# Attention scores on Trainium2: stacked heads formed on TensorE, or spread through DRAM by DMA

## The reference

```
x = x + fusion(recurrent layers(layernorm(x)))
s = layernorm(x)
q, k, v = s @ Wq + bq, s @ Wk + bk, s @ Wv + bv        # 16 heads of 8 features
scores = einsum('bqhd,bkhd->bhqk', q, k) * 8 ** -0.5
probs = softmax(scores)
attn = einsum('bhqk,bkhd->bqhd', probs, v) @ Wo + bo
x1 = layernorm(s + attn)
expert = floor(x1 @ router_w + router_b) mod 4          # one of four experts per token
x = x + layernorm(x1 + expert's MLP(x1))
```

## Time and profile before

| | us |
|---|---|
| median of 3 runs | 369.08 |
| lowest and highest of them | 367.32, 375.83 |
| profiled execution, its own time | 369.33 |
| its span, first to last instruction | 367.5 |
| TensorE busy in the span | 272.2 |
| VectorE busy | 247.6 |
| ScalarE busy | 191.5 |
| GpSimd busy | 145.1 |

### The profile page before, as it was taken

One profiled execution on the slowest core, in us unless ns is written; L12 is line 12 of the kernel. 1 busy time (PEld: TensorE's weight loads), 2 busy tenths in 40 slices (PEclk: granted clock), 3 DMA queues, 4 the chain that ended last, 5 costly groups with the idle time before them and its releaser, 6 DMA issues. The chain is left out here.

```text
span 367.5 us, 7953 instructions
## 1 busy us (share of the span) xinstructions
PE 272.2 (74%) x2807; PEld 197.3 (54%) x2807; DVE 247.6 (67%) x664; ACT 191.5 (52%) x357; POOL 145.1 (39%) x333
## 2 busy tenths in 40 slices
PE   2654686877876838759888888988865898679970
PEld 1233454545555524546557566756755757447860
DVE  5997788888888592263538656866864377728881
ACT  4323969979978764633654654465341233214420
POOL 1126547657557360131003301820420152726665
PEclk9966869989988985966999999999976699969995
...
GB/s 152 239 332 336 320 61 0 1 2 0 0 3 2 110 4 2 0 0 2 2 2 4 3 2 2 61 4 0 62 75 0 2 90 31 73 125 58 25 23 19
DMA packets 19806, 20.46 MB, mean 56 GB/s; under 512 B 1554, under 2 KB 18224, under 8 KB 19640
## 3 DMA queue, kind: packets, MB, share of 16 engines
...
## 5 line engine op out<-in xcount | busy, mean ns | idle before, releaser
L1128 ACT ACTIVATE probs<-scores 128x1024 f32<-128x1024 f32 x32 | 32.8, 1025 | 54.7 <-PE scores L801 54.4
L1392 DVE TENSOR_REDUCE mneg<-scores 128x8 bf16<-128x1024 f32 x32 | 39.0, 1218 | 24.7 <-PE scores L794 22.2
L1256 DVE TENSOR_TENSOR_SCAN early<-a_both,bank 128x512 f32<-128x512 f32 x32 | 38.8, 1212 | 4.5 <-issue 4.0
L428 POOL TENSOR_SCALAR a_both<-early 128x508 f32<-128x508 f32 x32 | 19.6, 611 | 37.6 <-ACT early L1025 33.7
L1400 DVE RECIPROCAL sums<-bank 128x128 f32<-128x128 f32 x16 | 15.3, 957 | 23.5 <-PE bank L824 23.4
L648 PE MATMUL scores<-ident,early 128*128 128x128 f32 x64 | 16.6, 319 | 17.7 <-DVE early L1274 16.3
L609 PE MATMUL bank<-ident,early 128*128 128x128 f32 x136 | 25.3, 318 | 5.0 <-ACT h_fwd L1042 2.1
L801 PE MATMUL scores<-mnegT,pick 32*128 32x128 bf16 x256 | 27.8, 239 | 0.0
L453 POOL TENSOR_TENSOR ln_tmp<-ln_tmp,minus_half 128x8 f32<-128x8 f32 x16 | 26.4, 1650 | 1.3
L1025 ACT ACTIVATE early<-scores,gate_wT 128x512 f32<-128x512 f32 x28 | 19.9, 712 | 11.0 <-PE scores L635 3.7
L648 PEld LDWEIGHTS scores<-ident,early 128*128 128x128 f32 x64 | 10.2, 167 | 28.0 <-issue 28.0
...
...
...
## 6 DMA issues: line engine op xcount, KB each, us to landing
...
late<-sorted_rows SPq DMA_DIRECT2D x15, 130.0 KB, 2.1
x_rows<-in_x_dram SPq DMA_DIRECT2D x4, 256.0 KB, 3.4
w_s<-in_L_ffn_W_dram SPq DMA_DIRECT2D x1, 1024.0 KB, 6.2
w_s<-in_L_ffn_W_dram SPq DMA_DIRECT2D x4, 256.0 KB, 6.8
a_both<-in_L_ffn_b_dram SPq DMA_DIRECT2D x1, 1024.0 KB, 4.7
x_rows<-sorted_rows SPq DMA_DIRECT2D x4, 130.0 KB, 2.0
ctx_rows<-in_ctx_dram SPq DMA_DIRECT2D x1, 256.0 KB, 2.9
```

Source lines behind the costliest of these rows:

```text
L428: pool.tensor_scalar(a_buf[d][:, (k // 2) % 2, :, keep], tiles(keep_buf[:, i, :])[:, :, keep], CLAMP_HI, CLAMP_LO, ALU.min, ALU.max).then_ ...
L1128: act.activation(probs[:, n % 2, 1 - h::2, :].rearrange("p (j i) q -> p j i q", i=2), exp_banks.rearrange("p i j q -> p j i q"), ACT.Exp, ...
L1256: dve.tensor_tensor_scan(out_s, a, b, 0.0, ALU.mult, ALU.add).then_inc(s["s_ready"], 1)
L1392: dve.tensor_reduce(mneg[:, n % 2, h::2, 0:4], max_banks, AX.X, ALU.max, negate=True).then_inc(s["mx_r"], 1)
```

## The change

Groups 1 to 3: no stacks on TensorE and ScalarE. SP writes each of k_hi, k_lo, q_hi and q_lo twice to DRAM (256 KB each, eight DMAs a group), at the places that the four planes have them in, waits for the four of the keys to land, reads the key stacks back with one 1 MB DMA (`k_in`), then does the same for the queries (`q_in`). The last score step's first half of a group waits for both.

Group 0: no stacks. ScalarE writes the keys in fp32 (`k_cols`), VectorE writes four copies of the queries in fp32, each with all features but those of one of every four heads set to 0 (`q_own`, mask `own`). `maxima_of` and `score_step` read them through `operands`, so that in tiles 0 to 3 the matmuls of lines 794 and 797 are fp32 (those of the maxima of tile 4, made at tile 3, are not). A head then stands at another place, and `exp_half` writes the first four tiles in that order. The `sel` matrices, which ScalarE zeroed and VectorE filled, are gone, and the work ahead of the loop is in another order. The diff, with most of the unchanged lines left out:

```diff
@@ -100,7 +100,7 @@
-        sel = sb("sel", [P, 4, NHEAD // 4, P], F32R)
+        own = sb("own", [P, 4])
         ctx_rows = sb("ctx_rows", [P, LAYERS, P])
@@ -145,6 +145,7 @@
                       for i, n in enumerate(("q_st", "k_st")))
+        q_own, k_cols = sb("q_own", [P, 4, CHUNK]), sb("k_cols", [P, CHUNK])
         v_z = sb("v_z", [P, TPC * NHEAD * VW + 3 * (VW + HD)])
@@ -184,6 +185,7 @@
         table = nc.dram_tensor("sorted_rows", [ROWS, ROW], F32)
+        k_spread, q_spread = (nc.dram_tensor(n, [NG - 1, NHEAD // 4, P, CHUNK], F32) for n in ("key_stacks", "query_stacks"))
         blank = sb("blank", [P, ROW])
@@ -225,12 +227,13 @@
         names = """x_in0 x_in1 x_in2 x_in3 ctx_in vec_in fw_in rw_in attw_in bc_in b12_in w1_in w2_in out_done
-        ident_done pool_init sel_z vz_z mask_done x_norm x_rowsT x_cols prep_T prep_cols
+        ident_done pool_init vz_z mask_done x_norm x_rowsT x_cols prep_T prep_cols
         u_ready keep_r gated b_r decay s_ready rows_ready st_r ln_p coef n_dve n_act cols_ready h_ready dve1
         fus_p fus_s fusT_p x1_r xn_r xnT_p xnT_s q_p q_hi_r q_lo_r k_p k_hi_r k_lo_r v_p v_r
-        ks_p ks_act qs_p qs_act xnb_r x1b_r norm_st_r norm_p norm_co_r
+        xnb_r x1b_r norm_st_r norm_p norm_co_r
         sc_p mx_r mT_p mT_s st_p exp_r pv_p att_r bv_c bvo_p bo_r wo_p r1_r xh1_r xh1T_p xaT_s key_p mask_r
         blank_r blanked consts cum_r rank_p place_r scattered0 scattered1 scattered2 scattered3 steer_r
+        k0_r q0_r k_out k_in q_out q_in
         xsT_p xs_r hid_p hid_r hidT_p relu_r y_p acc_r acc_p acc_rs_r o_r dve2""".split()
@@ -393,6 +396,24 @@
             sp.dma_start(b1_bc, b1.rearrange("(o e) f -> o (e f)", o=1).to_broadcast([P, NE * DFF])).then_inc(s["b12_in"], 16)
+            def spread_rows(g, dram, whole, rest, whole_at, rest_at, whole_r, rest_r, out, into, stacks):
+                spread = dram.ap()[g - 1].rearrange("j (i b d) c -> b (j i) d c", i=4, b=4)
+                for src, planes, ready in ((whole, whole_at, whole_r), (rest, rest_at, rest_r)):
+                    sp.wait_ge(s[ready], g)
+                    for b in planes:
+                        sp.dma_start(spread[b], src[:, :].bitcast(F32)).then_inc(s[out], 16)
+                sp.wait_ge(s[out], 16 * 4 * g)
+                sp.dma_start(stacks[g % 2][:, :, :].bitcast(F32), dram.ap()[g - 1].rearrange("j p c -> p j c")).then_inc(s[into], 16)
+            for g in range(1, NG):
+                if g == 1:
+                    sp.wait_ge(s["h_ready"], LAYERS * STEPS)
+                else:
+                    sp.wait_ge(s["st_p"], HALVES * TPC * (g - 1))
+                spread_rows(g, k_spread, k_hi, k_lo, (0, 1), (2, 3), "k_hi_r", "k_lo_r", "k_out", "k_in", k_st)
+                spread_rows(g, q_spread, q_hi, q_lo, (0, 2), (1, 3), "q_hi_r", "q_lo_r", "q_out", "q_in", q_st)
             for i in range(NS):
@@ -697,7 +718,7 @@
                 if g:
-                    pe.wait_ge(s["qs_act"], 4 * g)
+                    wait(pe, "q_lo_r", g - 1)
                     pe.wait_ge(s["h_ready"], LAYERS * STEPS)
@@ -706,6 +727,7 @@
                 pe.wait_ge(s["fus_s"], g + 1)
+                wait(pe, "k_lo_r", g - 1)
                 for t in range(TPC):
@@ -723,35 +745,6 @@
                 pe.matmul(dst[:, :], wq_s[:, :], xnT[:, :], start=True, stop=True).then_inc(s["q_p"], 1)
-            def stack_bank(g, j):
-                return bank[j] if g == 0 else bank[7 - j % 2]
-            def stack_keys(g):
-                for j in range(4):
-                    if j == 0:
-                        pe.wait_ge(s["k_lo_r"], g + 1)
-                    if j == 1 or g == 0:
-                        pe.wait_ge(s["q_lo_r"], g + 1)
-                    if j >= 2 and g:
-                        pe.wait_ge(s["ks_act"], 4 * g + j - 1)
-                    for lo, src in enumerate((k_hi, k_lo)):
-                        last = pe.matmul(stack_bank(g, j)[:, :], sel[:, lo, j, :], src[:, :], start=(lo == 0), stop=(lo == 1))
-                    last.then_inc(s["ks_p"], 1)
-            def stack_queries(g):
-                for j in range(4):
-                    if g == 0:
-                        pe.wait_ge(s["ks_act"], j + 1)
-                    elif j < 2:
-                        pe.wait_ge(s["ks_act"], 4 * g + 3 + j)
-                    else:
-                        pe.wait_ge(s["qs_act"], 4 * g + j - 1)
-                    for lo, src in enumerate((q_hi, q_lo)):
-                        last = pe.matmul(stack_bank(g, j)[:, :], sel[:, 2 + lo, j, :], src[:, :], start=(lo == 0), stop=(lo == 1))
-                    last.then_inc(s["qs_p"], 1)
@@ -764,15 +757,22 @@
+            def operands(g, rows, j, at):
+                if g == 0:
+                    return q_own[rows, j, at], k_cols[rows, at]
+                return q_st[g % 2][rows, j, at], k_st[g % 2][rows, j, at]
             def maxima_of(n, h):
...
                 for j in range(4):
+                    pe.wait_ge(s["q0_r"], j + 1)
                     for i in range(2):
                         rows, at = head_rows(h, i, t)
-                        last = pe.matmul(max_banks[:, i, j, :], q_st[g % 2][rows, j, at], k_st[g % 2][rows, j, at],
-                                         start=True, stop=True)
+                        q, k = operands(g, rows, j, at)
+                        last = pe.matmul(max_banks[:, i, j, :], q, k, start=True, stop=True)
                 last.then_inc(s["sc_p"], 1)
@@ -785,17 +785,17 @@
                     if t1 == 0:
-                        pe.wait_ge(s["ks_act"], 4 * (g1 + 1))
-                        pe.wait_ge(s["qs_act"], 4 * (g1 + 1))
+                        pe.wait_ge(s["k_in"], 16 * g1)
+                        pe.wait_ge(s["q_in"], 16 * g1)
                 for j in range(4):
...
                             rows, at = head_rows(h, i, t1)
-                            top = pe.matmul(max_banks[:, i, j, :], q_st[g1 % 2][rows, j, at], k_st[g1 % 2][rows, j, at],
-                                            start=True, stop=True)
+                            q, k = operands(g1, rows, j, at)
+                            top = pe.matmul(max_banks[:, i, j, :], q, k, start=True, stop=True)
                         rows, at = head_rows(1 - h, i, t)
-                        pe.matmul(exp_banks[:, i, j, :], k_st[g % 2][rows, j, at], q_st[g % 2][rows, j, at],
-                                  start=True, stop=False)
+                        q, k = operands(g, rows, j, at)
+                        pe.matmul(exp_banks[:, i, j, :], k, q, start=True, stop=False)
                     for i in range(2):
@@ -876,19 +876,17 @@
             keys(0, bank[1])
-            queries(0, bank[0])
-            to_cols(LAYERS - 1, STEPS - 2)
-            to_cols(LAYERS - 1, STEPS - 1)
-            pe.wait_ge(s["mask_done"], 3)
-            stack_keys(0)
-            stack_queries(0)
+            queries(0, bank[3])
             pe.wait_ge(s["bv_c"], 1)
             pe.matmul(bank[4][:, 0:P], bv_cols[:, :], wo_s[:, :], start=True, stop=True).then_inc(s["bvo_p"], 1)
-            pe.wait_ge(s["qs_act"], 4)
+            to_cols(LAYERS - 1, STEPS - 2)
+            pe.wait_ge(s["k0_r"], 1)
             maxima_of(0, 0)
+            maxima_of(0, 1)
+            to_cols(LAYERS - 1, STEPS - 1)
+            turn_shift(0)
             fusion(1)
-            maxima_of(0, 1)
-            turn_shift(0)
+            pe.wait_ge(s["mask_done"], 2)
             pe.wait_ge(s["pool_init"], 8)
@@ -912,8 +910,6 @@
                     router(g - 1)
-                if t == 2 and g < NG - 1:
-                    stack_queries(g + 1)
                 if t == 3 and g < NG - 2:
@@ -924,8 +920,6 @@
                     turn_xn(g + 1)
-                if t == 1 and g < NG - 1:
-                    stack_keys(g + 1)
                 if t == 1 and g == NG - 1:
@@ -998,8 +992,6 @@
             zeros = ident[:, :].unsqueeze(1)
-            act.activation(sel[:, :, :, :].rearrange("p a j c -> p (a j) c"), zeros.to_broadcast([P, NHEAD, P]),
-                           ACT.Identity, scale=0.0).then_inc(s["sel_z"], 1)
             act.wait_ge(s["prep_T"], 1)
@@ -1088,24 +1080,18 @@
                 act.wait_ge(s["k_p"], g + 1)
+                wait(act, "k_out", 16 * 4 * (g - 1))
                 act.activation(k_hi[:, :], src[:, :], ACT.Identity, bias=col(R_BK)).then_inc(s["k_hi_r"], 1)
...
                 act.wait_ge(s["q_p"], g + 1)
+                wait(act, "q_out", 16 * 4 * (g - 1))
                 act.activation(q_hi[:, :], src[:, :], ACT.Identity, bias=col(R_BQ)).then_inc(s["q_hi_r"], 1)
-            def stack_bank(g, j):
-                return bank[j] if g == 0 else bank[7 - j % 2]
-            def key_stacks(g):
-                for j in range(4):
-                    act.wait_ge(s["ks_p"], 4 * g + j + 1)
-                    act.activation(k_st[g % 2][:, j, :], stack_bank(g, j)[:, :], ACT.Identity).then_inc(s["ks_act"], 1)
```

(49 more changed lines are left out.)

## The result

The changed kernel takes 399.9 us (median of 4 runs, 397.91 to 403.02) against 370.9 for the kernel before beside it: a ratio of 1.086, interval 1.081 to 1.091. The forecast was 385.0 with a range of 373 to 397, so it had the direction, but the loss is nearly double, and outside the range. The profiled execution has a span of 396.5 us against 367.5, 29.0 more. Some executions of a kernel are a few per cent slower than the rest; all ratios here are of the faster ones, all medians of every execution.

What follows compares the result with a forecast made beforehand. It took TensorE's program order to bound a warm group. To 369.33 us it added 4.6 (boundary 1), 1.2 (tile 3 fp32), 4.0 (boundaries 2 and 3) and 6.0 (clock), +15.8, giving 385.1 us, range 373 to 397.

Steps and rivals of the forecast that it cites:

- The bound now, and what is removed: Warm groups: TensorE's program order bounds; removed key stacks held 2.5 us and query stacks 2.1, together 4.5 us a group.
- The chain of the round trip: Query writes, read and score step after the query remainder: 13.9 us to the exponential, +2.0 us at boundaries 2 and 3.
- high end for this term: DRAM round trip at boundaries 2 and 3 with every term at its slowest: +4.9 us over the 33.1 us beat.
- The order in the queue: SP's DMA queue: query write data stand behind the 1 MB key read and take 2.5 to 3.1 us after it.
- fp32 in group 0: Score steps of tiles 0 to 3: each +0.6 us at full clock, +1.2 at half; +3.5 before boundary 1, +1.2 after.
- The start: Work ahead of the loop, up to the first exponential: 1.3 us earlier, with ends -2.3 and 0.
- The clock: After TensorE's idle wait at each of three boundaries, half clock costs 2.0 us, +6.0 in all.
- the full 4.1 us each time: Upper cost of half clock after each boundary's stall; due every time, the total would be 6 us above the forecast.
- The clock rival: TensorE's clock stays at half from one boundary to the next: 395 to 402 us, chance 0.13.
- The hidden round trip: Groups 1 to 3: the DRAM trip costs no wait, so removed stacks pay: 360.5 us, chance 0.05.
- Rival 1: At the boundaries, the DMA chain ends at its low end and the clock holds: 372 to 376 us, chance 0.2.
- The signs: Expected in the trace: three query-read waits of 3 us or more, half clock after each, boundaries 35 to 38 us apart.

Runs made afterwards that it cites:

- run 7: Kernel before with the zero fill of sel moved later and only the keys of groups 1 to 3 through DRAM, query stacks on TensorE: ratio 0.999.
- Run 3: Changed kernel with SP issuing the four query writes ahead of the key read: ratio 1.054 against the kernel before.
- run 12: Kernel before with only 14 throwaway bf16 matmuls added in TensorE's waits in tiles 13 to 15: ratio 0.987, 364.1 us.
- Run 6: Kernel before with only ScalarE's zero fill of sel moved to a later place: ratio 0.999.
- run 4: Changed kernel with 42 throwaway bf16 matmuls on TensorE ahead of the wait at each boundary: ratio 1.066 against the kernel before.
- order with fillers: Changed kernel with the query writes ahead of the key read and 14 throwaway matmuls at each boundary: ratio 1.041 against the kernel before, 384.0 us.
- run 5: Changed kernel without key writes and key read, query stacks serving as both score operands in groups 1 to 3: ratio 1.041 against the kernel before.

## Why the prediction was wrong, step by step

**The bound now, and what is removed: right for the keys.** The key stacks were to hold 2.5 us of a group's path and the query stacks 2.1. With the keys' gone, chains went from 10.7 to 8.2 and from 11.85 to 9.9 us in the kernel of run 7; its middle one, 13.0, ran in part at the half clock shown above. No run takes away the query stacks without a DMA that ends later.

**The chain of the round trip: the step that failed.** The forecast had 13.9 us: query writes landed 7.3 after the remainder, the read 4.9, score step and handovers 1.7. Measured: 11.4, 5.2, 1.75, in sum 18.3. The last two terms were right. The first was off by 4.1: "1 MB more takes 2.5 to 3.1 us after the key read". Two parts of it show in the trace. The key read was issued 0.74 us after the remainder instead of 0.5 ahead of it: 1.2 us, from writes that SP sends in 0.6 us each, not in the 0.45 taken from the earlier trace rows, and that land 3.4 us after they are issued, not 2.7. Then the key read and the query writes took 10.65 us together (219.30 to 229.95) where 7.8 were forecast: I let 2 MB pass at the 418 and 336 GB/s of the earlier trace rows, which are single transfers in a steady stream, where the windows from 220 to 228 come to some 260 GB/s for the mix, and gave the landing of the last write nothing behind its bytes, while 2 us of near silence stand there. At boundary 1 it is 10.7, 5.4 and 2.9 us, 18.98 against 13.1: the score step there is fp32 and at half clock, and the "0.8 because the keys are further ahead" is not there, since the key read was issued 0.3 us after the remainder (175.52, 175.21).

My own high end for this term was +4.9 over before's beat and should have warned me: the measured excess is 6.4. The range took the bounds of each term but none for reads and writes in the same queue, the nearest rows being of one kind alone.

**The order in the queue: seen, but not priced.** The prediction said that the writes' data "stand in the same queue behind the key read", and then charged only their bytes. Run 3 shows that the place costs 4 us a boundary net, about 11.7 us in the time (3.2%, with 0.9% of uncertainty). That is about as much as the forecast was off by, 13 to 15 us. It is a coincidence that its chain, 14.3, is close to the forecast for the other order: in run 3 the read takes 7.3 us, not 4.9, and the writes land after 5.3, not 7.3.

**fp32 in group 0: right per step, too dear in sum.** A step at full clock, 153.50 to 154.83, is 1.33 us with its last pick's start (1.32 forecast); at half, 2.51 (2.64):

```profile
153.50 0.34 PE L795 MATMUL scores<-k_cols,q_own 32*128 32x128 f32 x1 [1.15 <-ACT mnegT L1109]
...
154.83 0.23 PE L801 MATMUL scores<-mnegT,pick 32*128 32x128 bf16 x2
```

```profile
191.27 0.44 PE L795 MATMUL scores<-second_stacks 32*128 32x128 f32 x1 [10.20 <-DMA second_stacks<-query_stacks]
...
193.78 0.32 PE L801 MATMUL scores<-mnegT,pick 32*128 32x128 bf16 x2
```

The stretch with the four steps ahead of the remainder grew by 1.4, not 3.5: the clock between 157 and 174 was 0.80 in that trace, against 0.60 in the kernel before. Alone, the half costs 0.5%, at most 1.3.

**The start: cannot be read from one trace.** -2.65 was measured, -1.3 forecast, but 2.2 of it already stand at the issue of the bias broadcast, where of all that the change touches only the zero fill of `sel` lies ahead (124.84 before, 122.65 after). In run 12, where the code up to tile 13 is the same as before's, that issue is at 121.47 and the first exponential at 152.18. So 5.6 us of start are the spread between executions. From that issue to the first exponential it is 32.9 before and 32.45 after, -0.5; but in run 12 it is 30.7, so this too lies inside the spread. Run 6, which was to test the removed zero fill, starts at 152.07 like run 12, which has the fill where it was, and is no faster than the kernel before.

**The clock: right in size, as far as the runs can tell.** 6.0 forecast; 7.6 from run 4, with 4 us of uncertainty; 5.1 from order alone to order with fillers, with 5. The ledger's 9.05 less 1.2 for fp32 leaves 7.9 behind the boundaries. In the prediction I had set beside it the warning of the Trainium skill, "TensorE: Matmul & The Clock Gate", section Why this matters for your kernels, that idle gaps between bursts bring the clock to half. The traces agree (0.50 in the wait at every boundary of the changed kernel), but the full 4.1 us each time that I worked out beside it, 12.3 in all, is more than any of these three figures. What I had not seen is that the kernel before pays for the same thing in its own last group.

**The rivals.** The clock rival (395 to 402, chance 0.13) names nearly the right time for a wrong reason: the clock was at 1.00 again 8 us after boundary 2 (245 to 253 us), and the fillers give back 5 to 8 us, not 10 to 17. The hidden round trip is excluded by run 5, where the chain is longer than the kernel before's even with half of the bytes. Rival 1, the low end with a held clock, fell to the chains of 18.3 us and the 0.50 in every wait.

**The signs.** The waits for the query read came three times and the half clock after each, as said; but the data reached TensorE 16.6 us behind the remainder (235.13 - 218.56) instead of 12 to 13, and the boundaries stood 42 to 43 us apart instead of 35 to 38. The first exponential, at 155.10, came a little ahead of the 156 to 158 forecast.
